# Unread TensorE products ahead of the attention scores of eight heads out of sixty-four

## The reference, cut to what matters

```python
xn = ln(x, g_norm)
q = (xn @ Wq).reshape(b, n, HEADS, DIM_HEAD).transpose(0, 2, 1, 3)      # 16 heads of 64
kv = xn @ Wkv                                                           # one key, one value head
...
sim = jnp.einsum('bhid,bjd->bhij', q, k) * SCALE
sim = sim + attn_bias
...
sim = jnp.where(causal, neg, sim)
attn = jax.nn.softmax(sim, axis=-1)
out = jnp.einsum('bhij,bjd->bhid', attn, v)
return ln(out @ Wout, g_out)
```

## Time and profile before

| | |
|---|---|
| time, median of 3 runs | 2487.56 us (2485.59 to 2491.07) |
| the profiled execution | 2490.37 us, its span 2488.6 us |
| mean granted TensorE clock over the span | 0.983 |
| busy: PE, PEld, DVE, ACT, POOL | 94%, 73%, 70%, 50%, 54% |

### The profile page before, as it was taken

One profiled execution on the slowest core, in us unless ns is written; L12 is line 12 of the kernel. 1 busy time (PEld: TensorE's weight loads), 2 busy tenths in 40 slices (PEclk: granted clock), 3 DMA queues, 4 the chain that ended last, 5 costly groups with the idle time before them and its releaser, 6 DMA issues. The chain is left out here.

```text
span 2488.6 us, 56588 instructions
## 1 busy us (share of the span) xinstructions
PE 2344.3 (94%) x20593; PEld 1818.2 (73%) x20593; DVE 1739.9 (70%) x4089; ACT 1237.4 (50%) x3133; POOL 1337.5 (54%) x1464
## 2 busy tenths in 40 slices
PE   5899999999999999889999999989899999999998
PEld 3677777777777777557777777757687877877876
DVE  4586777777777877578888887347674665755763
ACT  2676766666676766445555553124333333333332
POOL 3586777778786868266666666016332332322322
PEclk8999999999999999999999999999999999999999
DMA  4001210001010100011222212153111212111112
GB/s 147 18 27 30 64 40 28 27 28 34 22 36 27 29 23 23 22 23 40 49 57 58 57 38 57 39 163 94 39 60 44 73 56 60 55 58 60 60 35 61
DMA packets 192530, 122.10 MB, mean 49 GB/s; under 512 B 87728, under 2 KB 170672, under 8 KB 192256
## 3 DMA queue, kind: packets, MB, share of 16 engines
q1 hardware_dynamic: 166768, 79.74, 11.7%
q10 hardware_dynamic: 25488, 38.73, 5.2%
HBM read 97.29 MB, written 21.14 MB: 48 GB/s over the span
## 5 line engine op out<-in xcount | busy, mean ns | idle before, releaser
L1615 POOL TENSOR_TENSOR m_hid_part<-m_hid,m_hid_part 128x512 fp32r<-128x512 f32 x176 | 238.1, 1353 | 553.8 <-ACT m_hid_part L1524 550.5
L991 POOL TENSOR_TENSOR a_bm<-a_bias,a_mask_add 128x512 f32<-128x512 f32 (+3 forms) x512 | 438.2, 877 | 119.9 <-DVE a_nm L726 113.9
L902 ACT ACTIVATE a_S<-a_S,a_nm 128x512 f32<-128x512 f32 (+3 forms) x512 | 289.6, 566 | 231.6 <-DVE a_nm L726 226.9
L726 DVE CUSTOM_DVE_ANT_0 a_S<-a_S,a_bm,a_nsn 128x512 f32<-128x512 f32 (+3 forms) x512 | 276.4, 546 | 78.2 <-PE a_S L476 69.3
L1536 ACT ACTIVATE m_hid<-m_G 128x512 f32<-128x512 f32 x176 | 105.5, 599 | 390.1 <-PE m_G L1470 355.8
L476 PE MATMUL a_S<-a_kT,a_qT 128*128 128x384 f32 (+3 forms) x1024 | 284.6, 361 | 0.7 <-DVE a_nm L726 0.5
L1697 DVE TENSOR_TENSOR m_hid<-m_hid,m_U 128x512 f32<-128x512 f32 x176 | 121.1, 688 | 223.2 <-PE m_U L1470 189.6
L1487 PE MATMUL m_Y<-m_hid_part,m_down_high 128*128 128x512 f32 x704 | 256.5, 405 | 12.3 <-POOL m_hid_part L1615 11.5
L1470 PE MATMUL m_G<-m_in,m_gate_high 128*128 128x512 f32 x704 | 251.8, 398 | 0.9 <-POOL m_up_low L1609 0.9
L1470 PE MATMUL m_U<-m_in,m_up_high 128*128 128x512 f32 x704 | 250.7, 396 | 1.5 <-DVE m_hid L1697 1.2
L486 PE MATMUL a_T<-s_ident,a_S 128*128 128x128 f32 x1280 | 230.2, 278 | 19.4 <-ACT a_PT L911 15.4
(11 more groups left out here) (326 smaller groups left out, 5263.2 us busy)
## 6 DMA issues: line engine op xcount, KB each, us to landing
a_o<-s_weight_rows SPq DMA_DIRECT2D x128, 128.0 KB, 3.0
m_spread<-s_w ACTq DMA_DIRECT2D x64, 256.0 KB, 3.3
m_spread<-s_w ACTq DMA_DIRECT2D x128, 128.0 KB, 2.9
a_x<-in_x SPq DMA_DIRECT2D x32, 128.0 KB, 2.8
s_hT<-a_hT SPq DMA_DIRECT2D x32, 128.0 KB, 2.2
d_x<-in_x SPq DMA_DIRECT2D x8, 512.0 KB, 5.3
d_h<-s_hT SPq DMA_DIRECT2D x8, 512.0 KB, 5.6
s_xg<-d_xg SPq DMA_DIRECT2D x8, 512.0 KB, 3.1
```

The source lines that it names most:

```text
L726: dve.tensor_tensor_reduce(S[:, n % S_SLOTS, 0:w], SB[n % 2][:, 0:w], bm[:, n % BM_SLOTS, 0:w], -1.0, nsn[:, tile % 2, h:h + 1], ALU.add, ...
L902: act.activation(S[:, n % S_SLOTS, 0:w], S[:, n % S_SLOTS, 0:w], ACT.Exp, scale=-1.0, bias=nm[:, tile % 2, h:h + 1], accum_out=den[:, tile ...
L991: pool.tensor_tensor(bm[:, n % BM_SLOTS, 0:w], bias[:, h, L - w:L], mask_add[b % 2][:, 0:w], ALU.add).then_inc(s["bm_ready"], 1)
L1615: pool.tensor_tensor(hid_part[1][:, q % H_SLOTS], hid[:, q % G_SLOTS], hid_part[0][:, q % H_SLOTS].bitcast(F32), ALU.subtract).then_inc(hi ...
```

## The change

Ahead of the two score products of a head, and behind the wait for the bank, one more matmul is issued where n mod 64 is one of 11 to 18. It reads the identity as bf16, writes the columns of the same bank that the head does not use (`w` to 511) and nobody reads them. For heads 11 to 15 of a sequence's tile 0 these are 384 columns, for heads 0 to 2 of its tile 1 they are 256. There are 8 such heads in each of 8 sequences, so 64 added products.

```diff
+        WARM_HEADS = range(NH - 5, NH + 3)
...
+                def unread_beside(bank, w):
+
+                    words = ident[:].bitcast(BF16)
+                    pe.matmul(bank[:, w:].rearrange("p (a n) -> p a n", a=2), words[:, 0:P],
+                              words[:, 0:(L - w) // 2].unsqueeze(1).broadcast_to([P, 2, (L - w) // 2]), start=True, stop=True)
+
...
                             o_s = SB[n % 2]
+                            if n % (NH * TT) in WARM_HEADS:
+                                unread_beside(o_s, w)
                             for i in range(2):
                                 last = pe.matmul(o_s[:, 0:w], qT[:, tile % 2, h], kT[tile // TT % 2][i][:, 0:w],
                                                  start=i == 0, stop=i == 1)
```

## The result

Thirteen runs of each kernel gave a median of 2495.99 us for the changed one (2489.87 to 2502.49) and 2489.88 us for the one before (2484.69 to 2493.06). The ratio is 1.0028, 95% interval 1.0017 to 1.0040: slower by 0.28%, 4.2 to 10 us. A second set of twelve runs, on another occasion, gave 1.0020 (1.0010 to 1.0030). The forecast was 2491.8 us, +0.17%, with a range up to 2497.5. The kernel before measured 2489.88 us here and 2487.56 us when the forecast was built on it, so 2.3 of the 4.2 us between 2491.8 and 2495.99 are the baseline. Among the 29 executions of the kernel before beside the second set, one of 5466.26 us is slow and left out of every comparison.

What follows compares the result with a forecast made beforehand. PE sets the order of time from head 1 of tile 1, before it the cause alternates; seven sequences' 3.8 us plus 0.4 us in the first make 4.2 us on 2487.56, so 2491.8 us (+0.17%), range 2485.5 to 2497.5.

Steps and rivals of the forecast that it cites:

- in the open: Rival, chance 0.15: small waits on PE don't take in the products, all 64 show, 9.1 us more, 2496.7 us.
- Which products are covered: Second sequence: waits hide heads 11 to 13 and head 0 of tile 1; the other four show, 0.54 us.
- The price of one product: Each added product costs its stream of columns, 0.162 us for 384 and 0.108 for 256; its weight load is hidden.
- loads in the open: Rival, chance 0.03: each product adds its 0.097 us weight load at the four heads that show, 3.1 us more, 2494.9 us.
- The first sequence: Bias widening stands between its heads, PE waits 0.92 us behind head 15; cost 0.4 us, between 0.22 and 0.54.
- The clock: Products stand behind each clock fall in tile 0, their stretch already at full clock; effect valued at nothing.
- My price per piece: Tile 0, second against third sequence: a piece, 3.4 us at low clock, costs 0.96 us; eleven cost about 10.6 us.
- Hidden: Rival, chance 0.16: the next wait of each tile takes in the 0.54 us; 2487.6 us.
- Fewer falls: Rival, chance 0.12: lengthened sequences or the denser stretch avoid clock falls; 2481.2 us if all are gone.
- More falls: Rival, chance 0.08: each of seven sequences gets one more low-clock piece, 10.9 us in all, 2498.5 us.

Runs made afterwards that it cites:

- 32 columns: The changed kernel with each added product at heads 11 to 18 writing 32 columns instead of 384 or 256, weights still 128 columns; 1.0034 of the kernel before.
- early six: The changed kernel with its full products moved from heads 11 to 18 to heads 4 to 9 of tile 0; 0.9969 and 0.9965 of the kernel before.
- 32 by 32: The changed kernel with the products at heads 11 to 18 cut to 32 columns and their weights to 32 columns; 1.0059 of the kernel before.

## Why the prediction was right, point by point

**The sign and the range** held, and the size roughly: +4.2 us forecast, +7.0 and +5.0 us measured by the ratios, 2495.99 inside 2485.5 to 2497.5. It lies outside the 2489.8 to 2494 us that I gave the forecast by itself, though, and nearer to the 2496.7 us of "in the open". With both moved by the 2.3 us of the baseline, to 2494.1 and 2499.0 us, it stands between them; the time alone can't decide, the heads in the trace do.

**Which products are covered** was right head by head: 11, 12, 13 and 16 in waits, 14, 15, 17 and 18 in the open, 0.54 us forecast and 0.54 us in the mean of seven. For head 16 I named the wrong wait, the one before the projections instead of the one before its transposes. That what is late stays late was right too: behind head 3 of tile 1 each sequence takes the same time before and after (84.45 and 84.44 us in the second).

**The price of one product** was right in its sum and wrong in its reason, and that the sum came out is partly luck. I priced the stream, 0.162 and 0.108 us. In the second sequence heads 14 and 15 cost 0.30 us for a forecast of 0.32, heads 1 and 2 of tile 1 0.27 us for 0.22, and with 32 columns, whose stream I put at 0.014 us, the four still cost 0.46. The rule of the Trainium skill that I weighed ("TensorE: Matmul & The Clock Gate", Part 3: loads run beside a matmul only where the row group differs) is not borne out as it stands, since the product's load at 214.29 starts with the transpose before it, of the same 128 rows; but I was wrong to conclude from the 0.216 us pitch that an added product costs its stream alone. The rival "loads in the open", the stream and 0.097 us on top at each of four heads, asked for 0.93 us a sequence and is out as well.

**The first sequence** was mis-sized: 0.4 us forecast, 0.98 measured. Its heads 10 and 3 of tile 1 before:

```profile
84.27 0.63 PE L476 MATMUL a_S<-a_kT,a_qT 128*128 128x128 f32 x2
...
102.90 0.45 PE L476 MATMUL a_S<-a_kT,a_qT 128*128 128x256 f32 x2
```

and after:

```profile
85.47 0.63 PE L486 MATMUL a_S<-a_kT,a_qT 128*128 128x128 f32 x2
...
105.08 0.44 PE L486 MATMUL a_S<-a_kT,a_qT 128*128 128x256 f32 x2
```

18.63 and 19.61 us. With the widening of the bias between the heads, no wait covered the products of heads 11 to 15: the input transposes behind head 15 come 0.73 us later, counted from head 10 (11.53 against 10.80). I had set this sequence between 0.22 and 0.54 us by the wait behind head 15 and not priced the heads ahead of it. With it the direct cost is 3.8 + 1.0 = 4.8 us, inside both intervals (4.2 to 10 and 2.5 to 7.5 us).

**The clock** I valued at nothing, as four of eleven pieces more or less had no sign. Their number did not move (11; 11 and 12), but their place did, and it prices them. The falls of before that last 6.8 us cost 2.0 to 2.4 us over the 19.07 us that heads 0 to 10 take at full clock with the early six (without any product and any fall no profile shows them). In the changed kernel's fourth sequence the fall begins 13.3 us behind the first score, where those of before begin 12.1 to 12.7 us behind it, and 5.3 of its 6.8 us lie on the output projection (4.2 in the earlier trace rows, where the projection takes 5.76 us):

```profile
426.62 0.42 PE L486 MATMUL a_S<-a_kT,a_qT 128*128 128x128 f32 x2
...
441.36 6.34 PE L613 MATMUL a_F<-a_wout,a_oT 128*128 128x256 f32 x16
...
448.33 0.42 PE L486 MATMUL a_S<-a_kT,a_qT 128*128 128x128 f32 x2
```

21.71 us, 2.64 over 19.07. Added up over the seven sequences, falls cost 12.4 us before and 13.3 and 13.0 us in the two profiles of the changed kernel: 0.6 to 0.9 us more, from one profile of before. My price per piece, 0.96 us from the difference of two sequences, was low; 12.4 / 11 is 1.13. The direct 4.8 us and this make 5.4 to 5.7 us. The stretch with the products took 5.5 us more in the profile. What lies between that and the measured 5.0 and 7.0 is within the intervals, and I can't assign it: the rest of the kernel alone took 1479 to 1489 us in the thirteen profiles, by its own falls.

**The 32 by 32 kernel** fits this way of adding up: 7 x 1.26 us in its seven sequences, 2.1 us in the first (20.76 against 18.63) and 15.5 us of falls against 12.4 make 14.0 us, and 0.59% of 2488 us is 14.7 (10.7 to 18.7 by the interval).

**The rivals.** "Hidden" and "all in the open" are out by the table of heads. "Fewer falls" did not happen at these heads, but does a few heads earlier. "More falls", one more piece in each sequence, did not happen either: 11 and 12 pieces after 11. The Trainium skill, "TensorE: Matmul & The Clock Gate", Part 1, says that activity releases the throttle on the array's clock; the early six agree with it, 1.00 where 0.66 and 0.83 stood. For heads 11 to 18 there was nothing to release, their stretch stood at 1.00 before.

## What to carry to other kernels

Before adding work to keep TensorE's clock up, find in the trace the idle time just ahead of each fall and put it there. Six products ahead of heads 4 to 9 made this kernel 0.3% faster in two sets, and four ahead of heads 5 to 8 0.5% in a single set of five runs; eight of them at heads 11 to 18, where the clock had already come back, made it 0.2 to 0.3% slower. Don't price an added matmul by its columns, or by the pitch of a series of its own kind: put a narrow one in the same places and measure. And read head by head, in each variant of the loop, which wait covers it.

## What the runs showed of the hardware that I had not expected

- A bf16 matmul of 32 columns between fp32 ones costs PE 0.10 to 0.16 us where no wait covers it, as much as one of 256 columns in the same places (0.11 and 0.16); one of 384 costs 0.15 us.
- Weights of 32 columns between weights of 128 are dearer, not cheaper: 0.27 to 0.33 us for each product in the open. A change of the weights' shape shows as 0.20 us from a matmul to the next load.
- The falls can keep one place in the loop. In the 32 by 32 kernel a sequence takes 119.4 us, and each of the seven falls begins 12.3 to 12.5 us behind its first score and lasts 6.8 us (stretches from 199.0 and, the last, from 915.8; both wholly at 1.2 GHz):

```profile
199.00:205.60 6.60, 6.49 (x20) 4.65 (x20) 4.34 (x14) 2.92 (x11) 4.90 (x7) 0.50 0.02 5
...
915.80:922.40 6.60, 6.37 (x19) 4.71 (x19) 4.22 (x13) 2.92 (x11) 4.77 (x7) 0.50 0.00 1
```

In the other kernels, with sequences of 117 to 119 us, falls of 3.4 and 6.8 us mix and begin 11.6 to 15.0 us behind the first score. My reading, which no run tests by itself, is that a loop of suitable length meets the same place each time, and that a change of a few tenths of a microsecond moves it.
